# First layer of a four-layer image kernel: projections by blocks of 128 channels with moves to head rows, last image peeled; second layer: fp16 halves in a buffer of their own

## The reference, cut to what matters

```python
def _L0_conv_ref(x, w_qkv, w_proj, b_proj):
    qkv = jnp.einsum('oc,bchw->bohw', w_qkv, x)
    q, k, v = jnp.split(qkv, 3, axis=1)
    att = jnp.einsum('bhxd,bhyd->bhxy', q * scale, k)
    att = jax.nn.softmax(att, axis=-1)
    out = jnp.einsum('bhxy,bhyd->bhxd', att, v)
    return jnp.einsum('oc,bchw->bohw', w_proj, out) + b_proj[None, :, None, None]
```

```python
def deform_block(x, ow, ob, dw, pw, pb, K):
    offsets = conv2d(x, ow, ob, K // 2)
    out = deform_depthwise(x, offsets, dw, K, K // 2)
    return conv2d(out, pw, pb, 0)
```

## Time and profile before

| | us |
|---|---|
| median of 3 runs | 6949.88 |
| lowest and highest | 6949.5, 6953.95 |
| the profiled execution | 6961.99 |
| its span | 6960.2 |
| PE, DVE, ACT, POOL busy in it | 6208.9, 5077.9, 4105.7, 820.0 |

### The profile page before, as it was taken

How to read it: one execution, slowest core, us unless ns; L and a number is a source line. 1 busy time by engine, 2 the same in 40 slices (tenths; PEclk the granted TensorE clock), 3 DMA queues, 4 the chain that set the end, 5 groups by cost and what they waited for, 6 DMA issues and landing times. The chain is left out here.

```text
span 6960.2 us, 127532 instructions
## 1 busy us (share of the span) xinstructions
PE 6208.9 (89%) x47896; PEld 4197.8 (60%) x47896; DVE 5077.9 (73%) x10322; ACT 4105.7 (59%) x5626; POOL 820.0 (12%) x580
## 2 busy tenths in 40 slices
PE   6999999999997898998989989899898996999798
PEld 3444544444453556884567855678555785555598
DVE  7878888888895778896788867888778885333333
ACT  4766766676671556885567855678556883111242
POOL 3211221121122101001011010110001100000000
PEclk9999999999998999999999999999999998999898
DMA  3001001001002544545454544445444553000598
GB/s 119 26 25 34 17 27 34 17 26 34 25 17 81 126 105 118 118 111 124 104 120 111 118 118 104 113 116 119 105 118 106 123 119 100 37 36 36 131 232 195
DMA packets 182887, 617.14 MB, mean 89 GB/s; under 512 B 56585, under 2 KB 65217, under 8 KB 139379
## 3 DMA queue, kind: packets, MB, share of 16 engines
q1 hardware_dynamic: 182179, 607.94, 35.0%
HBM read 541.71 MB, written 65.59 MB: 87 GB/s over the span
## 5 line engine op out<-in xcount | busy, mean ns | idle before, releaser
L2334 PE MATMUL b_p<-b_work,b_hkt 64*128 64x144 f32 (+37 forms) x27520 | 2110.8, 308 | 259.0 <-DVE b_acc L2205 146.2
L2334 PEld LDWEIGHTS b_p<-b_work,b_hkt 64*128 64x128 f32 x27520 | 1959.7, 194 | 491.0 <-DVE b_work L2280 273.6
L2280 DVE TENSOR_TENSOR b_work<-b_work 128x140 f32<-128x140 f32 (+26 forms) x5312 | 1616.4, 355 | 246.8 <-PE b_p L2334 189.3
L2175 ACT ACTIVATE b_work<-b_work,b_mcol 128x512 f32<-128x512 f32 (+6 forms) x1328 | 765.6, 648 | 1061.5 <-DVE b_work L2280 903.1
L539 ACT ACTIVATE a_ex<-a_p_t 128x1024 f32<-128x1024 f32 x526 | 538.3, 1023 | 473.9 <-PE a_p_t L471 470.4
L2179 ACT ACTIVATE b_work<-b_work,b_mrow 128x544 f32<-128x544 f32 (+6 forms) x1328 | 762.6, 646 | 0.0
L2205 DVE SCALAR_TENSOR_TENSOR b_acc<-b_p,b_dwc,b_acc 128x323 f32<-128x323 f32 (+14 forms) x1088 | 622.6, 575 | 187.6 <-PE b_p L2334 187.6
L606 DVE TENSOR_REDUCE a_nm<-a_p_x 128x1 f16<-128x1024 f32 x537 | 654.9, 1219 | 119.2 <-PE a_p_x L460 114.4
L1747 PE MATMUL b_p<-b_hp,b_ow 128*98 128x512 f32 x1568 | 727.3, 615 | 0.0
L612 DVE TENSOR_TENSOR a_el<-a_ex,a_eh 128x1024 f16<-128x1024 f32 x525 | 664.5, 1266 | 11.2 <-issue 7.6
L544 ACT CAST a_eh<-a_ex 128x1024 f16<-128x1024 f32 x526 | 550.0, 1046 | 55.2 <-ACT a_ex L539 3.1
(11 more groups left out here) (219 smaller groups left out, 6409.5 us busy)
## 6 DMA issues: line engine op xcount, KB each, us to landing
b_work<-sampling_positions SPq DMA_DIRECT2D x666, 512.0 KB, 6.5
d_win<-merged_kernels SPq DMA_DIRECT2D x192, 263.0 KB, 6.8
b_xin<-x SPq DMA_DIRECT2D x24, 1024.0 KB, 9.9
a_xr<-in_x SPq DMA_DIRECT2D x12, 1536.0 KB, 7.5
a_xh<-in_x SPq DMA_DIRECT2D x9, 1536.0 KB, 6.7
x<-a_xr SPq DMA_DIRECT2D x9, 1536.0 KB, 5.8
c_xs<-x SPq DMA_DIRECT2D x9, 1536.0 KB, 6.4
b_xr<-x SPq DMA_DIRECT2D x13, 1024.0 KB, 19.7
```

The source lines that it names most:

```text
L2175: last = e.activation(rx[:, u, xo[c]:xo[c + 1]].rearrange("p (a b) -> p a b", a=H), pp[:, b, 1, :].rearrange("p (a b) -> p a b", a=H)[:, : ...
L2280: e.tensor_tensor(S[:, k % NS, 0:(r1 - r0) * w].rearrange("p (a b) -> p a b", b=w), rx[:, u, xo[cc]:xo[cc + 1]].rearrange("p (a b) -> p a ...
L2334: last = e.matmul(G[:, a0 - top:z0 - top, c0 - left:c1 - left], hkt[64 * s:64 * s + 64, SIDE * cr + cc, :], S[64 * s:64 * s + 64, k % NS, ...
```

## The change

In the first layer q and k are projected by three blocks of 128 channels and v by two sets of four heads, 20 units per image in place of 24, at slots that a table for the whole image gives. `high` and `low` write q and k by whole blocks into `split`, and `move` brings the pieces of a block to the rows of their heads by DMAs: rows 0 to 47 and 48 to 95 of `q` get the high and low half, and both row groups of `kh` and `kl` get a copy of k's. The maxima go to row 96. `high` waits, ahead of a block, until the moves of the block before have landed. `duplicate` and the zero rows are gone; `q`, `kh`, `kl`, `v` hold one image by heads. The units run further ahead, the loop goes over seven images, and the last is written out after it, without the steps and units of a ninth. In the second layer `hs` gets a buffer in which each half is contiguous. The weights of q and k come in the order of the blocks.

```diff
@@ layer0
-    QB = 4
     ER = 4
     WR = 4
-    UNITS = 6
     ROWS_OF = (0, 64)
-    MAXROW = D
+    MAXROW = 2 * D
+    SUMROW = D
     LEAD = 11
     BEHIND = 2
     FIRST = 14
-    UNIT_AT = (-12, -9, -6, -4, -1, 2)
+    BEGIN = -36
+    QUERY, KEY, VALUE = range(3)
+    UNIT = ([(s, 0, n) for s in (QUERY, KEY) for n in range(2)] + [(VALUE, 0, c) for c in range(4)]
+            + [(s, 1, n) for s in (QUERY, KEY) for n in range(2)] + [(s, 2, n) for s in (QUERY, KEY) for n in range(2)]
+            + [(VALUE, 1, c) for c in range(4)])
+    UNIT_AT = (28, 31, 34, 37, 40, 43, 45, 47, 50, 53, 56, 59, 62, 65, 78, 80, 82, 84, 86, 88)
+    UNITS = len(UNIT)
     OUT_AT = (71, 72, 73, 75, 76, 77)
-    JA = (2, 2, 2, 2, 1, 1)
-    PJA = sum(JA)
-    DUPS = 8
+    NORM_AT = 26
+    PIECES = [[(hd, max(P * j - D * hd, 0), min(P * (j + 1) - D * hd, D), max(D * hd - P * j, 0))
+               for hd in range(HEADS) if D * hd < P * (j + 1) and D * (hd + 1) > P * j] for j in range(G3)]
+    MOVES = [16 * 6 * len(pieces) for pieces in PIECES]
...
-        q = a.sb("q", [TP, QB, 2, N], F16)
-        kh = a.sb("kh", [TP, QB, 2, N], F16)
-        kl = a.sb("kl", [TP, QB, 2, N], F16)
-        v = a.sb("v", [P, 2, NT, 2, TP], F16)
+        split = a.sb("split", [P, 2, 2, N], F16)
+        q = a.sb("q", [MAXROW + 1, HEADS, N], F16)
+        kh = a.sb("kh", [MAXROW + 1, HEADS, N], F16)
+        kl = a.sb("kl", [MAXROW, HEADS, N], F16)
+        v = a.sb("v", [P, NT, HEADS, TP], F16)
         nm = a.sb("nm", [P, 4, NT], F16)
-        zr = a.sb("zr", [1, N], F16)
...
-                for whole in (kh, v, q, kl, zr, pj, o):
+                for whole in (v, o):
                     e.memset(whole[:], 0.0).then_inc(s_fill.sem, 1)
-                e.wait_ge(s_fill.sem, s_fill.at(7))
-                e.memset(kh[32:64, :, :, :], 1.0).then_inc(s_fill.sem, 1)
-                e.wait_ge(s_fill.sem, s_fill.at(8))
-                e.memset(v[:, :, :, :, MAXROW:MAXROW + 1], 1.0).then_inc(s_fill.sem, 1)
-                e.wait_ge(s_fill.sem, s_fill.at(9))
+                e.wait_ge(s_fill.sem, s_fill.at(2))
+                e.memset(kh[MAXROW:MAXROW + 1, :, :], 1.0).then_inc(s_fill.sem, 1)
+                e.wait_ge(s_fill.sem, s_fill.at(3))
+                e.memset(v[:, :, :, SUMROW:SUMROW + 1], 1.0).then_inc(s_fill.sem, 1)
+                e.wait_ge(s_fill.sem, s_fill.at(4))
...
+            s, j, n = UNIT[unit]
             if part == 0:
-                if unit == 0 and t == 0:
-                    e.wait_ge(s_h.sem, s_h.at(i // PAIRS + 1 if not isinstance(i, int) else 1))
+                if unit == 0:
+                    e.wait_ge(s_h.sem, s_h.at(i + 1))
                 e.wait_ge(s_jc.sem, s_jc.at(i * UNITS + unit))
-            if unit < 4:
-                s, n = divmod(unit, 2)
+            if s != VALUE:
                 for g in ((0,), (1, 2))[part]:
-                    last = e.matmul(p_j[0:TP, :], wqk[:, t, g, s, :], h[:, g, n * HALF:(n + 1) * HALF], start=(g == 0), stop=(g == G3 - 1))
+                    last = e.matmul(p_j[:], wqk[:, g, s, j * P:(j + 1) * P], h[:, g, n * HALF:(n + 1) * HALF], start=(g == 0), stop=(g == G3 - 1))
...
+                px, half = (2 * n + part) * P, HEADS // 2 * D
+                for g in range(G3):
+                    last = e.matmul(p_j[:, part * half:(part + 1) * half], h[:, g, px:px + P], wv[:, g, j * half:(j + 1) * half],
+                                    start=(g == 0), stop=(g == G3 - 1))
...
+        def high(e, i, unit):
+
+            s, j, n = UNIT[unit]
             held = pj[:, unit % 2, :]
-            if unit < 2:
-                e.activation(held[rows], p_j[rows], ACT.Copy, scale=SCALE).then_inc(s_jc.sem, 1)
+            if s != VALUE and n == 0:
+                e.wait_ge(s_block[j - 1].sem, s_block[j - 1].at((i + (j > 0)) * MOVES[j - 1]))
+            e.wait_ge(s_jc.sem, s_jc.at(i * UNITS + unit + 1))
+            if s != VALUE:
+                e.copy(split[:, s, 0, n * HALF:(n + 1) * HALF], held).then_inc(s_ja.sem, 1)
...
+        def low(e, i, unit):
+
+            s, j, n = UNIT[unit]
             held = pj[:, unit % 2, :]
-            e.wait_ge(s_jc.sem, s_jc.at(i * UNITS + unit + 1))
-            cols = slice(n * HALF, (n + 1) * HALF)
-            if unit < 2:
-                for hd, r in enumerate(ROWS_OF):
-                    e.copy(q[r:r + D, u, hd, cols], held[r:r + D, :]).then_inc(s_ja.sem, 1)
-            elif unit < 4:
-                for hd, r in enumerate(ROWS_OF):
-                    e.copy(kh[r:r + D, u, hd, cols], held[r:r + D, :]).then_inc(s_ja.sem, 1)
+            e.wait_ge(s_ja.sem, s_ja.at(i * UNITS + unit + 1))
...
+                e.tensor_tensor(split[:, s, 1, cols], held, split[:, s, 0, cols], ALU.subtract).then_inc(s_jv.sem, 1)
...
-        def duplicate(e, i, t, unit):
...
+        def move(e, i, s, j):
+
+            e.wait_ge(s_jv.sem, s_jv.at(i * UNITS + UNIT.index((s, j, 1)) + 1))
+            e.sem_inc(sh["tick"], 1)
+            for hd, d0, d1, r in PIECES[j]:
+                for part in range(2):
+                    rows = split[r:r + d1 - d0, s, part, :]
+                    if s == QUERY:
+                        e.dma_start(q[part * D + d0:part * D + d1, hd, :], rows).then_inc(s_block[j].sem, 16)
+                    else:
+                        for z in (0, D):
+                            e.dma_start((kh, kl)[part][z + d0:z + d1, hd, :], rows).then_inc(s_block[j].sem, 16)
...
-                        e.dma_start(q[MAXROW:MAXROW + 1, u, hd, :], zr[:]).then_inc(s_z0.sem, 16)
...
+                            move(e, b, KEY, 2)
+                        if not end:
+                            if hh == 3:
+                                move(e, b + 1, QUERY, 0)
+                            if hh == 4:
+                                move(e, b + 1, KEY, 0)
+                            if hh == 6:
+                                move(e, b + 1, QUERY, 1)
+                                move(e, b + 1, KEY, 1)
+                            if hh == 7:
+                                move(e, b + 1, QUERY, 2)
...
+                move(e, 0, QUERY, 0)
+                move(e, 0, KEY, 0)
+                move(e, 0, QUERY, 1)
+                row(0, 0)
+                move(e, 0, KEY, 1)
+                row(0, 1)
+                move(e, 0, QUERY, 2)
+                e.wait_ge(s_xr.sem, s_xr.at(16))
+                with e.Fori(0, B - 1) as b:
+                    image(b, False)
+                image(B - 1, True)
...
+                        for j in sorted({D * hd // P, (D * hd + D - 1) // P}):
+                            e.wait_ge(s_block[j].sem, s_block[j].at((b + k // STEPS + 1) * MOVES[j]))
...
-                for unit in range(UNITS):
-                    for part in range(2):
-                        project(e, 0, 0, unit, part)
-                for m in range(UNIT_AT[0], FIRST):
-                    slot(0, m)
-                with e.Fori(0, B) as b:
+                for m in range(BEGIN, FIRST):
+                    slot(0, m, False)
+                with e.Fori(0, B - 1) as b:
                     for m in range(FIRST, FIRST + STEPS):
-                        slot(b, m)
-                for bank in (p_o[2], p_o[1]):
-                    e.matmul(bank[0:TP, :], v[:, 0, 0, 0, :], eh[:, (FIRST - 1 - BEHIND) % WR, 0:HALF], start=False, stop=True)
+                        slot(b, m, False)
+                for m in range(FIRST, FIRST + STEPS):
+                    slot(B - 1, m, True)
@@ layer1
+        halves = a.sb("halves", [P, 2, 2, PW, PW], F16)
-        hs = hp[:].bitcast(F16).rearrange("p s a (b t) -> p s a b t", t=2)
+        hs = halves[:].rearrange("p t s a b -> p s a b t")
...
+            e.memset(halves[:], 0.0).then_inc(s_iv.sem, 1)
```

More of the change, by code:

```diff
@@ L213, in layer0 @@
         h = a.sb("h", [P, G3, N])
[L214 removed]
+        wqk = a.sb("wqk", [P, G3, 2, C])
         wv = a.sb("wv", [P, G3, C])
@@ L381, in norm, with unit_at @@
             last.then_inc(s_h.sem, 1)
-        def unit_at(m):
-            for t in range(PAIRS + 3):
+        def unit_at(m, end):
+            for ahead in range(0, 1 if end else 2):
                 for unit, r in enumerate(UNIT_AT):
-                    if m - 16 * t - r in (0, 1):
-                        return t + 1, unit, m - 16 * t - r
+                    if m - r + STEPS * (1 - ahead) in (0, 1):
+                        return ahead, unit, m - r + STEPS * (1 - ahead)
             return None
@@ L392, in order, with steps, ends_head @@
             return (1, 0) if k % NT == NT - 1 else (0, 1)
-        def where(k):
-            pair, hd, c = k // 16, k // NT % 2, k % NT
-            return pair % QB, pair % 2, hd, c
+        def steps(k, end):
+            return 0 <= k and not (end and k >= STEPS)
+        def ends_head(k, end):
+            return steps(k, end) and k % NT == NT - 1
         with nc.Block() as block:
@@ L511, in slot @@
```

(25 more changed lines are left out.)

212 lines of the change are left out of this document (84 added, 128 removed).

## The result

| us | before | after |
|---|---|---|
| median | 6949.69 | 6784.15 |
| ratio, 95% interval | | 0.976 (0.9745 to 0.9774) |
| the profiled execution | 6961.99 | 6786.86 |
| its span | 6960.2 | 6785.1 |

The change brings 165.5 us by the medians. The forecast was 6713, 237 less than before.

What follows compares the result with a forecast made beforehand. PE was taken to bound the kernel (DVE in slots without projection); seven periods -147, start 0, last image -69, second layer -23 and +2 for clearing sum to -237, from 6949.88 to 6713 us, range 6650 to 6815.

Steps and rivals of the forecast that it cites:

- Per image, PE: First layer, each image: q and k projections 96 to 72 passes, -10.3 us; v 192 to 96 passes, about -6 us.
- Per image, DVE's relief: First layer, each image: DVE relieved of 24 us; half of PE's 14.8 us idling ending with DVE goes, -7.5 us.
- Per image, the new wait: First layer, slot 64: ACT's cast of q's third block waits 4.6 us for the second block's moves; PE loses +3.5 us.
- -20.3: First layer, each image: the unrounded sum of PE, DVE's relief and the new wait, taken as -21 us.
- The rival that DVE holds the period: First layer: free slots cost 2.48 to 2.6 us, PE keeps its idling, period gains 8 us not 21; 6804; chance 0.24.
- Start: First image: more units ahead (about +6 us), free slots (-9) and ACT's wait once (+4), nothing in sum.
- Last image: First layer's last image, peeled with nothing projected for a ninth: 187 us in place of 255.9, -69 us.
- Second layer: Convolution's 1360 matmuls read adjacent fp16: step costs 0.021 us each, 29 us, four fifths on PE's path, -23 us.
- The rival that the step costs nothing: Second layer: the 0.034 us belongs to windows' edges, passes stay at 0.250 us; 6736 us; chance 0.20.
- Slower by SP's queue: Rival: moves hold SP longer than 0.51 us, lengthening ACT's wait; gain gone at 2.6 us, 6993 at 3; chance 0.06.
- The signs: Right: stores 228 to 229 us apart, ACT waiting 3 to 5 us, issues 0.5 us; wrong: stores above 235 apart.

Runs made afterwards that it cites:

- the run with small subtractions: Changed kernel with the projection's subtractions (split and v) cut to 64 or 48 columns, other low halves left out: 6783.98 us, 0.975 of the kernel before.
- The run with own semaphores: Changed kernel with one semaphore for q's moves and one for k's in each block: 6732.67 us, 0.9682 of the kernel before.

## Why the prediction was right, and where not

The sign, the range and the largest parts held; the point was 71 us too low. By the steps of the prediction:

- *Per image, PE: -16.3.* Right. Without the new wait PE is busy 212.9 us of a period (mean of seven), 18.6 less than before; part of the surplus may be the clock, 0.99 in place of 0.98. Passes are 72 and 96. All of it reached the period.
- *Per image, DVE's relief: -7.5.* Too large. PE's idling fell by 3.6 (18.1 to 14.5, means of seven), of which 3.0 is the wait for the normalised image. DVE gave less than the 24 us, too: its splits of whole height took 0.86 us and not 0.69, those of v 0.82 and not 0.55, so it took back 17.0 in place of 12.6. I took half of all idling that ends with DVE. But it stands in a few places, at the statistics (4.0 of 11.4 us) and the ends of heads, each behind work that comes in one piece there. Less work elsewhere does not shorten these, as the run with small subtractions showed.
- *Per image, the new wait: +3.5.* The step that was furthest off. The wait on ACT is as I worked it out, 4.99 us against 4.6 (an issue takes 0.63 and not 0.51, so sixteen take 10.1; the landing is shorter). I then let PE's own work cover part of it. It covers almost nothing, 4.46 us reach PE, and the clock takes 2.6 more. The run with own semaphores puts it at 8.1 us a period (235.6 - 227.5), 7 of it in that slot. So -18.6 - 3.6 + 8.1 = -14.1 stands where I had -20.3.
- *The rival that DVE holds the period.* It gives 6804 with 8 us an image, and the time lies nearer to it than to my forecast, but its cause is not what happened: slots without projection took 2.17 us where no end of a head was near (scores at 1041.46 and 1043.63), not 2.48, since DVE has caught up in the slots around them.
- *Start: 0.* It was +6.4; the same wait on ACT stands there too, since without it the first store comes at 143.6.
- *Last image: 187.* From the scores at 1795.77, where the prediction's 255.9 also begins, it took 192.5, 5 more; that the 187.7 of the table meets the 187 is chance. The output products, the bare chain (PE waits 10.2 us for POOL) and the statistics are about as listed. The 27 slots bounded by DVE are not: they took some 77 us with their ends of heads, where I had 67 + 4.5. And peeling was worth less in all than in this layer, see the second layer.
- *Second layer: -23 for the step.* The number held by luck, by two errors that cancel. The step costs 0.031 us a matmul, not 0.021 (the rows of 128x512 in the first layer, 0.216, were the right measure), so 1360 x 0.031 = 42, of which 34.5 reached the end in the kernel before: four fifths, as put. And the place of PE's code against its blocks, which the changed first layer moved, gives back 14 us of them (20.1 in place of 34.5), and some 22 to 25 against the best offset measured. That was in no step.
- *The rival that the step costs nothing*, and with it the rule of the page "SBUF — State Buffer", section "Door 1", of the Trainium skill: falls. A step of two fp16 is well within its eight, and 41 matmuls fit in 10 us in place of 47.
- *Slower by SP's queue: no.* A move holds SP for 0.63 us, far from 2.6, and 36 more of them an image cost nothing in the period.

The signs: the stores are 235.6 apart, just over the 235 that I had named as wrong, and not 228 to 229. ACT's wait (4.99 us), the passes, and 47 matmuls in 10 us are as named for right; a move's issue took 0.63 and not 0.5.

## What to carry to other kernels

When idling ends with an engine, list where it stands before taking a share of it: a lower average load does not shorten a wait behind one piece of work. A stall of PE is to be costed with the lower clock after it: here 4.46 us of standing cost 7.1, and 2.56 cost 4.2, 1.6 times their length each. And a counter that lumps two groups of transfers makes the earlier user wait for the later group; give each its own.

## What the hardware showed that I had not expected

- Where PE's program lies against the 16 KB blocks of its fetching is worth 23 to 25 us here (6786 to 6761 by 80 instructions that do nothing, 6692 to 6669 by 67). A change in the code of one layer can so move another by more than the 0.2% that this kernel's measurement can tell. Four offsets occur in these runs (41, 53 or 54, 121, 240); no others were tried.
- An issue of a move between two rows of SBUF costs SP 0.63 us, whether for 16 or 48 rows and for 1024 or 512 columns (six in 3.7 us, eight in 5.0).
- What a loop's turn costs DVE shows only when the work before it is moved away: 2.44 us, and about 4 us in PE's two slots after it.
